# Quantized attention: four blocks turned into one, in a kernel of four attention and feed-forward layers

## What is computed

```python
def _w8a8_linear(x, w, b):
    qx, sx = _dyn_quant(x)      # s = max|row| / 127, q = clip(round(x / s))
    qw, sw = _quant_weight(w)
    return jnp.einsum('bnc,oc->bno', qx, qw) * (sx * sw[:, 0]) + b
q = _w8a8_linear(x, wq, bq)     # 16 heads of 16 channels
k = cond @ wk.T + bk
v = cond @ wv.T + bv
scores = jnp.einsum('bhnd,bhld->bhnl', q, k) * inv_sqrt_d + mask[:, None]
o = jnp.einsum('bhnl,bhld->bhnd', jax.nn.softmax(scores, axis=-1), v)
return _w8a8_linear(o, wo, bo)
```

## Time and profile before

| | |
|---|---|
| median of 3 runs | 1227.47 us (1227.47 to 1230.66) |
| profiled execution | 1230.68 us, its span 1228.9 us |
| mean granted TensorE clock | 0.933 |
| busy, share of span | PE 1073.5 us (87%), DVE 913.5 (74%), ACT 780.6 (64%), POOL 546.6 (44%) |
| the attention that is changed | 871.4 to 981.3 us of the span |

### The profile page before, as it was taken

How to read it: one execution, slowest core, us unless ns; L and a number is a source line. 1 busy time by engine, 2 the same in 40 slices (tenths; PEclk the granted TensorE clock), 3 DMA queues, 4 the chain that set the end, 5 groups by cost and what they waited for, 6 DMA issues and landing times. The chain is left out here.

```text
span 1228.9 us, 20831 instructions
## 1 busy us (share of the span) xinstructions
PE 1073.5 (87%) x6796; PEld 761.8 (62%) x6799; DVE 913.5 (74%) x1737; ACT 780.6 (64%) x1228; POOL 546.6 (44%) x736
## 2 busy tenths in 40 slices
PE   4888956699889978999789999999777688999998
PEld 3545523444568855555668888888434476888886
DVE  5667887624767767888877777777758877777777
ACT  5567867489557745777456777666554455767774
POOL 7243547003536603126436666664120156666662
PEclk8788967799999988999989999999879799999999
DMA  6763120477224316432134453332010011433342
GB/s 180 223 191 104 42 81 1 111 203 198 69 76 129 110 31 187 137 112 71 32 101 126 124 192 121 121 123 75 23 27 1 7 33 42 123 119 119 119 119 73
DMA packets 74143, 125.21 MB, mean 102 GB/s; under 512 B 10401, under 2 KB 43873, under 8 KB 73431
## 3 DMA queue, kind: packets, MB, share of 16 engines
q1 hardware_dynamic: 72342, 117.87, 32.9%
q0 software_dynamic: 864, 6.03, 1.4%
q10 hardware_dynamic: 864, 0.39, 0.1%
HBM read 108.21 MB, written 15.45 MB: 101 GB/s over the span
## 5 line engine op out<-in xcount | busy, mean ns | idle before, releaser
L2130 POOL TENSOR_TENSOR f_up_lo<-f_w_up,f_up_hi 128x1024 fp32r<-128x1024 f32 (+1 forms) x70 | 164.7, 2352 | 162.3 <-ACT f_up_hi L1980 162.3
L1135 ACT ACTIVATE a_probs<-a_p_sc 128x1024 f32<-128x1024 f32 x192 | 189.4, 1019 | 29.0 <-PE a_p_sc L1007 21.6
L1279 DVE TENSOR_REDUCE a_maxes<-a_p_max 128x2 f32<-128x512 f32 x256 | 160.1, 682 | 50.4 <-PE a_p_max L974 50.0
L1007 PE MATMUL a_p_sc<-a_q,a_k 75*128 75x256 bf16 (+1 forms) x768 | 118.9, 282 | 11.4 <-DMA a_q<-a_neg_t 6.4
L1812 PE MATMUL f_p_y<-f_hid_hi,f_down_hi 128*128 128x512 f32 x304 | 120.9, 398 | 4.1 <-DVE f_hid_lo L2284 1.9
L1812 PE MATMUL f_p_y<-f_hid_lo,f_down_hi 128*128 128x512 f32 x304 | 119.7, 394 | 0.0
L1812 PE MATMUL f_p_y<-f_hid_hi,f_down_lo 128*128 128x512 f32 x304 | 119.3, 392 | 0.0
L1028 PE MATMUL a_p_out<-a_probs,all_v 128*32 128x256 f32 x1536 | 111.8, 402 | 0.3 <-ACT p_out L1143 0.3
L1007 PEld LDWEIGHTS a_p_sc<-a_q,a_k 75*128 75x128 bf16 (+1 forms) x768 | 68.9, 100 | 60.0 <-ACT a_probs L1135 21.7
L2249 DVE TENSOR_TENSOR f_p_u<-f_p_u,p_x_t 128x512 f32<-128x512 f32 x67 | 46.9, 699 | 79.0 <-PE f_p_u L1798 78.9
L974 PE MATMUL a_p_max<-a_k,a_q 72*128 72x256 bf16 x512 | 91.4, 292 | 15.2 <-DMA a_q<-q_parts 8.4
(11 more groups left out here) (411 smaller groups left out, 2765.5 us busy)
## 6 DMA issues: line engine op xcount, KB each, us to landing
f_coef<-coef SPq DMA_DIRECT2D x43, 512.0 KB, 3.6
f_w_up<-in_w SPq DMA_DIRECT2D x70, 256.0 KB, 3.0
a_q<-q_parts SPq DMA_DIRECT2D x48, 288.0 KB
f_w_down<-in_w SPq DMA_DIRECT2D x76, 128.0 KB, 2.0
a_k<-k_plain SPq DMA_DIRECT2D x96, 96.0 KB
a_k<-k_unit SPq DMA_DIRECT2D x24, 192.0 KB
outs<-p_out SPq DMA_DIRECT2D x32, 128.0 KB, 1.9
p_whole<-outs SPq DMA_DIRECT2D x32, 128.0 KB, 2.6
```

Source lines behind the costliest of these rows:

```text
L1007: last = nc.tensor.matmul(p_sc[pair % 2][:, h % 2, t * D:(t + 1) * D], k_of(b, h, K_ROWS)[:, t * P:(t + 1) * P], q_of(b, h, K_ROWS), start ...
L1135: nc.scalar.activation(probs[b % 2][:, 2 * pair:2 * pair + 2, :, :].rearrange("p h t d -> p h (t d)"), p_sc[pair % 2][:], ACT.Exp, scale=s ...
L1279: nc.vector.tensor_reduce(maxes[b % 3][:, :, h], p_max[:, n % 3, :].rearrange("p (t d) -> p t d", t=NK), axis=AX.X, op=ALU.max, negate=Tru ...
L2130: nc.gpsimd.tensor_tensor(up_lo[slot(t, 2)][:, 0:width], w_up[slot(t, 2)][:, 0:width], up_hi[slot(t, 2)][:, 0:width], ALU.subtract).then_i ...
```

## The change

The four blocks become one block in which every tile goes through query projection, scores, softmax, output projection in a software pipeline.

- Keys: ACT writes two masked copies (even and odd head of a pair of heads) in place of eight. Queries: the transposed queries are written four times per tile by ACT (two 128-column halves, each with two masks, with bias and weight scale applied as per-partition operands). Scores: sixteen matmuls of 64 rows x 64 x 128 columns per tile in place of four of 128 x 64 x 512.
- Values: per batch item and parity, two matmuls of 128 columns and a third that adds the bias; ACT copies the values out, not DVE.
- The largest values of the weight rows are found in the feed-forward of layer 2 (`measure_weights`), and `m.scale_ready` tells of it.
- Six of the eight tiles are normalised by ACT (`apply_by_act`), two by DVE.
- The loop order is written out in the diff, for each engine. PE and ACT have per iteration i: the transposes and products of the queries of tile i+3, the scores of tile i+2, the probabilities of tile i+1, the output projection of tile i-1.
- PSUM: `p_s`, `p_p` two banks, `p_o`, `p_q`, `p_y`, `p_t` one each, so all are held by one tile at a time.

```diff
+            @block.tensor
+                for i in range(NI + 1):
+                    if i + 3 < NI:
+                        turn_x(i + 3)
+                        queries(i + 3)
+                    if i + 2 < NI:
+                        scores(i + 2)
+                    if i + 3 < NI:
+                        turn_q(i + 3)
+                    if i + 1 < NI:
+                        turn_probs(i + 1)
+                        weigh(i + 1)
+                    if i >= 1:
+                        turn_o(i - 1)
+                        outputs(i - 1)
+            @block.scalar
+                copy_values(3)
+                whole_x(3)
+                exps(0)
+                copy_probs(0)
+                whole_weights(1)
+                copy_weights(1)
+                for i in range(NI + 1):
+                    if i + 3 < NI:
+                        copy_x(i + 3)
+                        scale_q(i + 3)
+                        copy_q(i + 3)
+                    if i + 1 < NI:
+                        exps(i + 1)
+                        copy_probs(i + 1)
+                    if i >= 1:
+                        whole_o(i - 1)
+                        copy_o(i - 1)
+                    if i + 4 < NI:
+                        whole_x(i + 4)
+                    if i in (3, 4):
+                        front.split_high(act, lambda out, src: copy(out, src, ACT.Copy), i - 3)
+            @block.vector
+                soften(0)
+                for i in range(NI + 2):
+                    if i + 1 < NI:
+                        soften(i + 1)
+                    if i + 4 < NI:
+                        quantize_x(i + 4)
+                    if 1 <= i <= NI:
+                        quantize_o(i - 1)
+                    if i < NI:
+                        divide(i)
+                    if i >= 2:
+                        emit(i - 2)
```

The start of PE and ACT, ahead of that loop, and the functions it calls:

```diff
+                def values(b):
...
+                    for odd in range(2):
+                        for k in range(NK):
+                            nc.tensor.matmul(bank[64 * odd:64 * odd + 64, at:at + P], cond[:, k, b * L:(b + 1) * L],
+                                             wv[:, k, :].rearrange("p (q s c) -> p q s c", s=2, c=XC)[:, :, odd, :],
+                                             start=(k == 0), stop=False)
+                        last = nc.tensor.matmul(bank[64 * odd:64 * odd + 64, at:at + P], bc(m.ident[:, 0:1], [0, L]),
+                                                bias_v[:].rearrange("p (q s c) -> p q s c", s=2, c=XC)[:, :, odd, :],
+                                                start=False, stop=True)
...
+                def scores(i):
+                    pe.wait_ge(q_copied, i + 1)
+                    pe.wait_ge(k_copied, 4 if i < NI // 2 else 8)
+                    if i >= 1:
+                        pe.wait_ge(masked, 2 * i)
+                    for k in range(NK):
+                        for j in range(2):
+                            for r in range(2):
+                                rows = slice(64 * r, 64 * r + 64)
+                                for b2 in range(2):
+                                    last = nc.tensor.matmul(
+                                        p_s[r][64 * b2:64 * b2 + 64, (2 * k + j) * P:(2 * k + j + 1) * P],
+                                        q_t[i % 2][rows, k, j, 64 * b2:64 * b2 + 64],
+                                        k_pairs[rows, k, 2 * i + b2, :, :].rearrange("p h l -> p (h l)"),
+                                        start=True, stop=True)
...
+                for g in range(4):
+                    keys(g)
+                turn_weights(0)
+                turn_x(0)
+                two_values(0)
+                queries(0)
+                two_values(1)
+                turn_q(0)
+                turn_x(1)
+                two_values(2)
+                queries(1)
+                scores(0)
+                two_values(3)
+                turn_q(1)
+                two_values(4)
+                turn_x(2)
+                two_values(5)
+                queries(2)
+                scores(1)
+                two_values(6)
+                turn_q(2)
+                two_values(7)
+                turn_probs(0)
+                weigh(0)
+                turn_weights(1)
...
+                def copy_q(i):
+                    act.wait_ge(q_turned, i + 1)
...
+                    for k in range(NK):
+                        for j in range(2):
+                            last = copy(q_t[i % 2][:, k, j, :], p_q[:, D + k * P:D + (k + 1) * P], ACT.Identity,
+                                        bias=bq_own[:, k, j:j + 1], scale=w_own[:, k, j:j + 1])
+                    last.then_inc(q_copied, 1)
...
+                norm.table(act, m.ident)
+                norm.scalar(act)
+                act.wait_ge(b_loaded, 6 * 16)
+                act.wait_ge(bk_ready, 1)
+                copy_keys(0)
+                whole_weights(0)
+                copy_keys(1)
+                act.wait_ge(norm.shift_ready, 1)
+                for i in range(BY_VECTOR, NI):
+                    norm.apply_by_act(i)
+                whole_x(0)
+                copy_weights(0)
+                copy_x(0)
+                copy_keys(2)
+                scale_q(0)
+                whole_x(1)
+                copy_q(0)
```

More of the change, by code:

```diff
@@ L54, in align @@
         if gap:
-            self.sb("gap", [P, gap // 4])
+            self.sb(f"gap{self.nc.sbuf_base}", [P, gap // 4])
     def over(self, name, shape, dt, at):
@@ L430, in place_last_attention @@
     m.cond = part(4 * NK * D, T)
+    m.w_largest, m.w_deq, m.w_factor = [part(4 * NK * D + NK * T + 4 * n, 2) for n in range(3)]
 def load_last_attention(sp, m, a):
@@ L2339, in third_gate, with measure_weights @@
                     low_sum(0)
+                def measure_weights():
+                    dve.wait_ge(m.raw_loaded, 32)
+                    for n in range(2):
+                        last = nc.vector.tensor_reduce(m.w_largest[:, n, :], m.raw[n][:], axis=AX.X, op=ALU.max,
+                                                       apply_absolute_value=True)
+                    link(last)
+                    link(nc.vector.tensor_scalar(m.w_deq[:], m.w_largest[:], 1.0 / 127.0, 1e-8, ALU.mult, ALU.max))
+                    nc.vector.reciprocal(m.w_factor[:], m.w_deq[:]).then_inc(m.scale_ready, 1)
                 v = nc.vector
@@ L2468, in _ @@
                 low(NT - 1, 1)
+                if layer == 2:
+                    measure_weights()
                 dve.wait_ge(y_done, 2)
@@ L2977, in token_scale @@
     link(nc.vector.reciprocal(factor, deq))
+BY_VECTOR = 2
+VALUES = 4
 def quantized_attention(nc, m, a, front):
[L2982 to L3013, removed]
[L3014 to L3382 removed]
@@ L3415, in program @@
         m.cond_loaded = st.sem("cond_loaded")
+        m.scale_ready = st.sem("scale_ready")
         early = ExitStack()
@@ L3520, in layout @@
     arrays["xk_w"], arrays["xv_w"] = width_first(I["L3_xattn_wk"].T), width_first(I["L3_xattn_wv"].T)
-    arrays["xq_b"], arrays["xo_b"], arrays["xv_b"] = I["L3_xattn_bq"], I["L3_xattn_bo"], I["L3_xattn_bv"]
-    arrays["xk_b"] = I["L3_xattn_bk"].reshape(NK, P).T
-    arrays["own"] = (p[:, None] // XC == np.arange(8)[None]).astype(f)
+    arrays["xo_b"], arrays["xv_b"] = I["L3_xattn_bo"], I["L3_xattn_bv"]
+    arrays["xk_b"], arrays["xq_b"] = I["L3_xattn_bk"].reshape(NK, P).T, I["L3_xattn_bq"].reshape(NK, P).T
+    of_head = np.stack([p // XC % 2 == 0, p // XC % 2 == 1, p // (2 * XC) % 2 == 0, p // (2 * XC) % 2 == 1], 1)
+    arrays["own"] = of_head.astype(f)
     arrays["cond"] = width_first(ctx.reshape(T, D).T)
```

681 lines of the change are left out of this document (363 added, 318 removed).

## The result

The changed kernel takes 1245.4 us, the median of four runs (1242.9 to 1247.9), against 1227.5 (1225.6 to 1230.7) for the kernel before: a ratio of 1.0144, interval 1.0113 to 1.0174. It is slower by 18 us. Forecast were 1243.4 us and a range of 1223 to 1256. A second measurement of the same kernel, further down, gave 1.0118 (1.0090 to 1.0146).

What follows compares the result with a forecast made beforehand. Before, DVE was nearest to a bound; in the new loop, a serial chain of PE and ACT. Full-clock sum 2.1 us plus low clock 0.67 x 20.6 gave +15.9 on 1227.5: 1243.4 us, range 1223 to 1256.

Steps and rivals of the forecast that it cites:

- the front: Block's start until iteration 0 begins, with keys, values and first exponential: ends at 920.1 at full clock, 922 at low.
- steady tile: One loop iteration, an unbroken chain of PE and ACT: 9.6 us at full clock, 12.5 at low; DVE needs 7.5.
- values, two items, full clock: Value products before the loop: three of one parity in a row overlap only at seams, 2.1 to 2.3 us.
- iterations 0 to 4 (low): The loop's iterations containing the query part: 61.7 us at the low clock, 47.2 at full.
- tail (low): From iteration 5 to the block's end: 20 us at the low clock, 15.8 at full.
- the lower bound of 0.85: `scores` in the loop: 0.85 us if four quadrants work at once; 1.2 was taken, upper end 1.94.
- rival 3: Loop's clock low throughout, `scores` quadrants only in pairs, 3.4 us at low clock: +32 us, 1255; chance 0.06.
- values finished well before 37 us: Sign against the forecast: value products done well before 37 us into the block.
- for how long the clock is low: Loop's clock: low two thirds of the time, from layer 0's feed-forward mean of 0.67; 0.67 x 20.6 us.
- +22.7: Front, loop and tail all at the low clock: end at 1003.7, 22.7 us later than before.
- The rival on which I had put 0.20: Loop's clock is back after an iteration and stays: +2 us, within -3 to +6, 1229.5; chance 0.20.
- the faster rival: `scores` 0.85, values 1.72 per pair, `copy_q` 0.25 per instruction; chain about 8.5 us: -8 us, 1219.5; chance 0.10.

Runs made afterwards that it cites:

- filler run: Changed kernel plus idle matmuls for PE, 12 per tile between `turn_q(i+3)` and `turn_probs(i+1)` and 30 ahead of `turn_probs(0)`: 1232.8 us, ratio 1.0018.
- the reordered one: Changed kernel with `exps(i+1)` ahead of the query's scaling and copies on ACT, `turn_probs(i+1)` ahead of `turn_q(i+3)` on PE: 1224.7 us, ratio 0.9955.
- the alternating parities: Changed kernel with value products issued in alternating parity (k outside, odd inside, bias products last): 1245.9 us, ratio 1.0110.
- the last kernel with fillers in the tail: Changed kernel with both lists reordered, `exps(0)` moved up, value products alternating in parity, idle matmuls in iterations 5 to 7: 1216.3 us, ratio 0.9877.
- plain copies: Changed kernel with `copy_q` as plain copies, without per-partition bias and weight scale: 1245.8 us, ratio 1.0110.

## Why the prediction was right

The sign, the cause and the size came out as forecast: a chain of PE and ACT, at the low clock, 12.5 us forecast and 12.46 measured. The total, though, is near by luck: it rests on two errors that offset each other. Point by point (times of the front from the block's start; where two values stand, the first is at the full clock and the second at the low one):

| Step | forecast | measured |
|---|---|---|
| steady tile | 9.6 / 12.5 us | some 9.15 (estimate, filler run) / 12.46 |
| `turn_x` to `queries` | 0.86 / 1.0 | 0.77 / 0.90 |
| `scores`, to the next product | 1.2 / 1.9 | 1.03 / 1.91 |
| `copy_q` | 1.6 | 1.51 |
| `turn_probs` to `weigh`, `weigh` itself (low) | 2.58, 1.95 | 2.75, 1.93 |
| values, two items, full clock | 2.1 to 2.3 | 1.73 |
| values ended, from the block's start | 40.5 | 35.9 |
| first exponential | 44 or later | 39.0 |
| iteration 0 begins (low) | 50.5 | 46.1 |
| iterations 0 to 4 (low) | 61.7 | 59.7 |
| tail (low) | 20 | 20.1 |
| clock behind the front | low two thirds | low nearly throughout |
| block, against before | +15.9 | +16.0 |

**What held.** `measure_weights` costs nothing, as said: it runs from 863.09 on with no idle time ahead of it, and the copy at 864.92 has none either, where DVE had stood 1.75 us. `scores` at 1.03 us lies between the 1.2 taken and the lower bound of 0.85; rival 3, with 3.4 us, is out. PE's stand ahead of the first `turn_probs` is the 4.1 us in the waits above, as forecast. DVE stands in each tile and PE ends the wait.

**`scores`, and the change of tiling mode.** The 1.2 us were taken from `weigh` by the number of instructions (the 64 columns that the forecast gives them are those of the array; 34 are streamed). `weigh` takes 1.06 us for 32 instructions at full clock and `scores` 1.03, but that they agree is chance. In `scores` the first four instructions start within 0.02 us of each other and the next fours follow after 0.16 and then every 0.11 us, the pace of one half of the array in the value products: the four quadrants work at once. Eight such steps are 0.87 us, the lower bound of the forecast. The rest is the change of mode, which can be seen. In the changed kernel `turn_q` stands behind `scores`, in the reordered one behind `turn_probs`, a product of its own mode:

```profile
932.53 0.38 PE L3187 MATMUL c_p_q<-all_ident,c_q 128*128 128x128 f32 x2
```

There it starts 0.11 us after the last instruction before it and its second instruction 0.11 us after its first. Behind `scores` the two are 0.20 and 0.17 us (0.44 us in all for the pair at 896.68), and at the low clock 0.35 and 0.27, against 0.21 and 0.21. So this change into 128x128 costs some 0.15 us at full clock and 0.19 at the low one. The Trainium skill (TensorEngine Tiling (Array Packing), Key Properties) says that a change of mode drains TensorE and that different tiles work in parallel. The trace agrees with both, with the pause of 0.15 us and the four quadrants at once. The forecast's sum had done without a price for the change; it is small, and the kernel before had such changes too.

The two operands of `copy_q` cost (12.1 - 6.3) / 32 = 0.18 us per instruction. The Trainium skill (ScalarE: Activation LUTs, What ACT_TABLE_LOAD costs) gives some 93 ns for each per-partition operand, and the difference of the two groups agrees with it.

**The step that failed first: the front.** It was forecast 4.4 us too long. The last bias lands, and DVE goes on, at 875.76, 5.7 us into the block, where 6.5 were forecast; PE is then 3.03 us behind the weights' copy instead of 3.8; and a pair of value items takes 1.73 us and not 2.2. Over eight pairs that alone is 3.8 us; with the transfer's 0.8 it is the whole error. My argument was that three products of one parity in a row can't overlap and only the seams can. The first part holds: one half takes 0.22 us per product, as the forecast's 0.213 says. The second failed: the other half starts its products before the first has done its three, as the rows under the alternating parities show, so a pair takes six products in a row (1.31 us), 0.16 at the start of the group and 0.26 for the half that is behind. That this is as much as before (1.72) is chance: there it was four products of 256 columns for each half. By the forecast's own list "values finished well before 37 us" spoke against it; they ended at 35.9.

**The step that failed second: for how long the clock is low.** I took two thirds from layer 0's feed-forward. It is nearly the whole loop. With it low from end to end the forecast's own numbers gave +22.7. The front takes 4.4 us off that, the two iterations that were partly at the higher level 1.4 (the first took 10.4 us and the fifth 11.9, where the three between took 12.4 to 12.5), and small terms 0.6, among them the 0.4 for `split_high`, which didn't show. That is +16.3, and measured were +16.0. So the step on the clock took 6.8 us off where 1.4 were right, and the front and the small terms were 5.0 us too long: two errors of some 5 us lay against each other in the 1243.4. A feed-forward whose DVE is busy 0.85 of the time was the wrong neighbour for a chain in which all three stand; the row at 0.50 with a 2.78 us wait for the exponential was the right one, and I had used it only for durations.

**Not counted.** The feed-forward behind begins at the low clock and costs 2.6 us more than before; the forecast had named 2 us of it and put them at nothing, behind the filler matmuls. Over the profiled executions it goes with the clock there: 247.6 us before, where it was never low behind the block, 248.5 in the last kernel with fillers in the tail, and 249.4 to 251.1 in all others, which began that stage low.

The rival on which I had put 0.20, a clock that comes back and stays, is what the filler run makes true for the most part, by force: 1232.8 us, 1229.5 forecast. Of the faster rival's three terms one came true, the values at 1.73 us, if not by its reason; `scores` at 1.03 and `copy_q` at 0.38 per instruction (1.51 / 4) did not, and the chain stayed over its 8.6 us. What does bring it under is another order of the lists, which I had not looked for.

## What to carry to other kernels

Write out each engine's in-order list for one steady iteration and ask of every wait whether the data needs it or only the list: here PE stood 2.5 us per tile behind `copy_q` and `exps`, filling that wait with idle work gave back 12 to 15 us through the clock, and swapping lines turned a loss of 1.2 to 1.4% into a gain of 0.5%. Where no engine is full, look for a chain: in this one 0.73 us per tile came back at nearly full length, and once DVE was full the same saving didn't show. Cut the block of two executions into front, loop and tail before you credit an edit with the difference: a part that it doesn't touch moved by 3 us with the clock. And for the clock of a loop that isn't there yet, look in the trace of before for a stretch with the same wait in PE's work, not for one with the same kind of work.

## What the runs showed of the hardware that I had not expected

- The level of the clock followed the loop and not its entry. Entered at 0.53, a loop without the 2.5 us wait was granted 1.00 from its second tile on; the loop with the wait was twice at 1.00 and fell back to 0.50 each time. With waits of 1.81 us (plain copies) it was still 0.50 to 0.71; with 1.23 us behind fillers 0.76 to 1.00. Adding work that nobody needs shortened the kernel.
- Value products that fill half of the array run side by side with those of the other half even where three of one half stand in a row: 12 of them take 1.73 us so, and 1.47 alternating, at the same clock. Within one half they don't overlap (0.22 us each; 2.56 us if the halves didn't overlap either). Products of 64 rows and 64 columns ran in all four quadrants at once, an instruction in each every 0.11 us. Both are read from the order and the starts of the instructions.
- A change from 64x64 into the tiling mode 128x128, ahead of an f32 product, costs 0.15 us at the full clock and 0.19 at the low one.
- The start of the block, which none of the edits to the changed kernel touches, lay between 869.5 and 874.6 us in the profiled executions. A cut of 2 to 5 us in one stretch can be read off the trace and yet be lost in the median of four runs.
